# Early ternary of the gate weights inside the first attention, and the tail's weight transposes moved ahead

## The reference, cut to what matters

```
x = x + attention(layernorm(x), ctx, ctx)          # 16 heads, 1024 keys, causal
x = x + mixture_of_experts(layernorm(x))           # 8 experts, top 2, hidden 1024
x = x + quantised_attention(layernorm(x), ctx)     # Wq, Wkv, Wp; all 2048 keys
x = x + ternary_ffn(layernorm(x))                  # w_gate, w_up (2048 x 512), w_down (512 x 2048)

def weight_quant(w):
    s = 1.0 / clip(mean(abs(w)), 1e-5)
    return clip(round(w * s), -1.0, 1.0) / s
```

## Time and profile before

| | us |
|---|---|
| median of 3 runs | 1581.54 |
| lowest, highest | 1578.25, 1591.35 |
| the profiled execution's own time | 1582.63 |
| its span, first to last instruction | 1580.7 |
| busy: PE, DVE, ACT, POOL | 1310.6, 1212.1, 997.3, 335.0 |
| mean granted clock of PE | 0.903 of full speed |

### The profile page before, as it was taken

One profiled execution on the slowest core, in us unless ns is written; L12 is line 12 of the kernel. 1 busy time (PEld: TensorE's weight loads), 2 busy tenths in 40 slices (PEclk: granted clock), 3 DMA queues, 4 the chain that ended last, 5 costly groups with the idle time before them and its releaser, 6 DMA issues.

```text
span 1580.7 us, 24025 instructions
## 1 busy us (share of the span) xinstructions
PE 1310.6 (83%) x8549; PEld 768.5 (49%) x8596; DVE 1212.1 (77%) x1799; ACT 997.3 (63%) x1291; POOL 335.0 (21%) x317
## 2 busy tenths in 40 slices
PE   8992888888865799999999997655777777779886
PEld 3441455555534566666666664313343444444333
DVE  6998899999976655555666664876999999984963
ACT  5775788888853455544455551335889888882574
POOL 1113200000004444445552004001112111110440
PEclk9996999999987899999999999766888778779998
DMA  8996455445344899999999975399887789783001
GB/s 293 288 288 164 94 114 133 121 117 122 79 167 190 327 416 417 414 417 418 415 415 403 354 273 173 65 204 212 174 170 171 162 164 177 164 145 96 1 1 53
DMA packets 453868, 338.65 MB, mean 214 GB/s; under 512 B 367464, under 2 KB 369512, under 8 KB 453136
## 3 DMA queue, kind: packets, MB, share of 16 engines
q1 hardware_dynamic: 439488, 291.31, 63.6%
q0 software_dynamic: 9920, 37.75, 6.3%
q10 hardware_dynamic: 4368, 8.39, 1.4%
HBM read 205.86 MB, written 38.01 MB: 154 GB/s over the span
## 4 chain that ended last, share of the span: by engine, by line
PE 37%; DVE 29%; issue 16%; DMA 7%; ACT 5%; POOL 3%; SPq 2%; POOLq 0%; DVEq 0%; ACTq 0%
DVE arena L2066 12%; PE scores L1137 8%; DMA arena<-in_L_ffn_w 5%; PE bank L1169 4%; PE scores L1236 4%; PE bank L1019 4%; PE scores L1003 2%; DVE arena L1836 2%; PE bank L1283 2%; DVE arena L1822 2%; PE scores L1002 2%; ACT arena L1480 2%; PE scores L1265 1%; PE bank L1381 1%; POOL xs_d L861 1%
## 5 line engine op out<-in xcount | busy, mean ns | idle before, releaser
L2066 DVE TENSOR_SCALAR_CACHE_REDUCE arena<-scores,arena 128x1024 f32<-128x1024 f32 x256 | 314.4, 1279 | 45.2 <-PE scores L1236 44.3
L1920 DVE TENSOR_TENSOR wlo<-raw,whi 128x2048 fp32r<-128x2048 f32 x92 | 219.8, 2409 | 157.8 <-ACT whi L1531 157.8
L1610 ACT ACTIVATE arena<-arena 128x2048 int16<-128x2048 f32 x128 | 273.5, 2149 | 74.9 <-POOL arena L902 39.3
L1236 PE MATMUL scores<-arena 96*128 96x512 bf16 x512 | 193.3, 485 | 85.3 <-DVE arena L2066 77.9
L1531 ACT ACTIVATE whi<-raw 128x2048 fp32r<-128x2048 f32 x92 | 173.2, 1908 | 51.1 <-PE scores L1137 51.1
L1169 PE MATMUL bank<-arena 128*128 128x512 f32 x368 | 163.8, 594 | 4.0 <-DMA arena<-in_L_ffn_w 3.9
L1137 PE MATMUL scores<-whi,xhi 128*128 128x512 f32 x368 | 159.3, 433 | 3.8 <-DVE xlo L1924 2.1
L1137 PE MATMUL scores<-whi,xlo 128*128 128x512 f32 x368 | 146.3, 398 | 0.0
L1137 PE MATMUL scores<-wlo,xhi 128*128 128x512 f32 x368 | 146.2, 397 | 0.0
L1480 ACT ACTIVATE arena<-scores 128x512 f32<-128x512 f32 (+3 forms) x256 | 116.6, 506 | 26.2 <-PE scores L1003 26.2
L1822 DVE TENSOR_REDUCE arena<-scores 128x1 f32<-128x640 f32 (+3 forms) x128 | 127.6, 1018 | 4.8 <-PE scores L980 4.4
(11 more groups left out here) (292 smaller groups left out, 2336.3 us busy)
## 6 DMA issues: line engine op xcount, KB each, us to landing
raw<-in_L_ffn_w SPq DMA_DIRECT2D x92, 1024.0 KB, 13.2
arena<-in_L_ffn_w SPq DMA_DIRECT2D x46, 1024.0 KB, 18.4
arena<-arena SPq DMA_DIRECT2D x32, 256.0 KB, 2.9
kst_d<-arena POOLq DMA_DIRECT2D x16, 384.0 KB, 5.6
tern_d<-arena POOLq DMA_DIRECT2D x12, 512.0 KB, 6.8
arena<-kst_d SPq DMA_DIRECT2D x16, 384.0 KB, 4.0
xs_d<-arena SPq DMA_DIRECT2D x23, 256.0 KB, 2.9
arena<-xs_d SPq DMA_DIRECT2D x22, 256.0 KB, 16.4
```

Source lines behind the costliest of these rows:

```text
L1236: ins = pe.matmul(scores[:, s:s + 512], qhead[h % 2][0:K3, t * P:(t + 1) * P], khead[h % 2][0:K3, s:s + 512], start=True, stop=True)
L1610: act.activation(dst, src, ACT.Exp, bias=ebias[n % SBUFS], scale=-1.0, accum_out=rsum[h % 2][:, t:t + 1]).then_inc(p_ready, 1)
L1920: dve.tensor_tensor(wlo[:, n % SPLITS], raw[:, n % RAWS], whi[:, n % SPLITS].bitcast(F32), ALU.subtract).then_inc(lo_done, 1)
L2066: dve.tensor_scalar(ssb[i][:, s:s + 1024], scores[:, s:s + 1024], nsq[:, h, t:t + 1], None, ALU.mult, ALU.min, accum_out=nmx[i][:, half:ha ...
```

## The change

The first four chunks of the ternary (all of the gate weight) are made in the first attention. Each gets six units: its load is cut into four quarters of 256 KB, two after the last `p2` group of one unit and two after the same group of the next; a unit is left out; then one step of three in each of the next three units. The first load waits for the fourth unit's last group, the last step for the 27th unit's. The other eight chunks stay where they were, behind the scatter.

The transpose of the gate weight is issued once the last expert slot's hidden rows are turned (`h_turned`), the transpose of the up weight behind the key loads that follow `moe_added`; both are gone from the place behind L693.

```diff
-TERN_EARLY = 0
+TERN_EARLY = 4
...
             sp.dma_start(bq_row, bq.partition_broadcast(P)).then_inc(wq_loaded, 16)
 
+            def turn_weights(w):
+                sp.dma_start_transpose(wT[w].rearrange("p o c n -> p (o c) n"), tern_d[w]).then_inc(wT_in, 16)
+
+            sp.wait_ge(h_turned, 2 * SLOTS)
+            turn_weights(0)
...
             sp.wait_ge(moe_added, 3 * NT)
             load_keys(0)
             load_keys(1)
+            turn_weights(1)
...
             load_queries(1)
-            for w in range(2):
-                sp.dma_start_transpose(wT[w].rearrange("p o c n -> p (o c) n"), tern_d[w]).then_inc(wT_in, 16)
             sp.dma_start(wp_sb, Wp.rearrange("(k p) n -> p k n", p=P)).then_inc(wp_loaded, 16)
...
+            def at_unit(u):
+                pool.wait_ge(p2_done, 4 * (TERN_UNIT + u))
+
             def load_chunk(g, chunk):
                 w, c = g // 4, g % 4
-                if w < 2:
+                if g < TERN_EARLY:
+                    for o in range(4):
+                        at_unit(6 * g + o // 2)
+                        pool.dma_start(chunk[:, o * D:(o + 1) * D], w_rows[w][(4 * c + o) * P:(4 * c + o + 1) * P, :]).then_inc(w_in, 16)
+                elif w < 2:
...
             def in_window(g, i):
 
                 if g < TERN_EARLY:
-                    pool.wait_ge(p2_done, 4 * (TERN_UNIT + 3 * g + i))
+                    at_unit(6 * g + 3 + i)
...
-                pool.wait_ge(w_in, 16 * (g + 1))
+                pool.wait_ge(w_in, 16 * (g + 1 + 3 * min(g + 1, TERN_EARLY)))
```

## The result

The changed kernel takes 1573.02 us (median of 7 runs, 1569.15 to 1576.32), the kernel before in the same series 1581.49 (7 runs). The ratio is 0.9939, with a 95% interval of 0.9924 to 0.9954: 9.6 us, or 0.6%, faster. (The two medians are 8.5 us apart; gains are given by the ratios here, and the interval makes this one 7.3 to 12.0 us.) The forecast was 1563.2, and 18.3 us. So about half of the expected gain came, and the time lies at the upper end of the range of 1557 to 1573, 0.02 us past it. The profiled execution has 1573.34 us, a span of 1571.5 and a clock of 0.908.

A forecast was written before the change was run, and what follows sets the result against it. DVE bounds both attentions, PE with the DMA engines the middle of the experts, plus a hole at 1057 to 1078 us. 17.0 + 3.1 - 1.0 - 0.3 - 0.5 = 18.3 us gain off 1581.5: 1563.2 us, range 1557 to 1573.

The forecast's parts named there:

- The hole: Second attention, 1057 to 1078 us: PE and DVE wait behind SP's two weight transposes; moving them gains 17.0 us.
- Less load beside the experts: Expert stage: four fewer ternary chunks return four slots from 20.10 to 19.32 us, gaining 3.1 us.
- Ternary steps in the first attention: POOL's 12 steps of 1.90 us fit a 2.3 us window in DVE's order; cost 0.5 us for all.
- The up transpose behind the keys: Before the queries: SP is free just in time for the first query transpose; cost 0.3 us, bounds 0 and 8.4.
- The gate transpose at the end of the experts: Beside the 16 gathers: the transpose delays the last gather little; cost 1 us, upper bound 8.2.
- B: Only the hole goes: POOL's lighter stream frees nothing and gathers cost 3; gain 13.2 us, 1568.3; chance 0.15.
- A: Query stage: the up transpose delays the queries, price 6.3 us; gain 12, time 1569.5; chance 0.12.
- C: First attention: POOL's 12 steps each hold DVE 1.90 us, 22.8 in all; 4.0 us slower, 1585.5; chance 0.04.

The follow-up runs named there:

- the experiment with the other window: Changed kernel with the gate transpose behind the gathers and each early ternary step released two `p2` groups earlier: 1572.19 us, one run.
- the experiment with two transposes: Changed kernel with both weight transposes issued behind the key loads, before the first query transpose: 1570.11 us, ratio 0.9907.

## Why the prediction was right and wrong

- **The hole: right.** Forecast 17.0 us, measured 16.9 up to the issue of the first probability transpose and 17.2 up to PE's products. That transpose landed in 7.23 us instead of 7.52, and PE's idle time went from 21.19 to 3.63; I had given 4 to 5 for it.
- **Less load beside the experts: right.** 3.1 us forecast, 3.4 by the marks, 3.0 for the whole ternary part alone. The slots that came back are the four between 781 and 862 us. The value chunks' slots moved up by four and keep their excess, as forecast: 701.02 to 780.94 is 79.9 us for four. Eight early chunks returned no more than four, since one collision of a value chunk with DVE cost PE 3.33 us there.
- **Ternary steps in the first attention: right.** 0.5 forecast, 0 to 0.1 measured. The way it was found, a window of 2.3 us in DVE's order against a step of 1.90, holds, and the experiment with the other window gives its worth: 12 to 13 us. By the Trainium skill, "SBUF — State Buffer", Who interferes with whom, DVE's reductions from PSUM don't ask for the shared ports and its subtractions of two SBUF inputs do; the two placings agree (1.90 us a step against 2.58 to 3.04).
- **The up transpose behind the keys: right.** 0.3 forecast, none measured. It took 9.65 us instead of 8.2, so the first query transpose came 2.0 us after DVE's tile was ready (1021.8), but the third was on time again at 1030.93. The slack that the forecast read from the earlier trace rows was enough for 2 us, and the experiment with two transposes shows that 18.5 us of issue are not absorbed.
- **The gate transpose at the end of the experts: wrong, and by nearly the whole miss.** "I take 1" turned out as 12.3 us, and so the upper bound, "all its 8.2 us go in front of the last gather", was too low as well. The step that failed is this: I took 8.2 us, an issue time measured away from the gathers, for what the transpose costs beside them, added it to 15 us of gather work, and found that 23 fit into 24. Already alone the transpose takes 10.0 us to land, and beside the gathers its packets' time does not stay what it was: 9.5 became 20.3, and the gathers' 14.8 became 16.6. That is 36.9 us of packet time where the forecast had counted 23, and the last gather landed after 17.0 us instead of 3.5. The hint was in the earlier trace rows: in the window of the hole the engines, with the two transposes, stand at a share of 1.14 for 271 GB/s, where the experts' loads get 415 out of 1.03. A transfer that fills the engines at so low a rate is not one that fits between others. I read this row for the hole and not as the transpose's price.
- The Trainium skill's rule, that all issuing engines share the same 16 DMA engines and interleave ("DMA: Bandwidth & Descriptors", Issuing engines are not separate DMA queues), is borne out, from POOL's queue and from ACT's: beside loads from either the transpose issues in 16.3 and 16.8 us instead of 8.0. The 1 to 2 us that I worked out by it came from adding times, which is my step and not the rule's.

With 12.3 in place of 1.0, and the other terms as forecast, the sum would be 17.0 + 3.1 - 12.3 - 0.3 - 0.5 = 7.0 us, 1574.5; measured are 9.6 and 1573.0. Of the rivals, B had "the gathers cost 3", on the right place with a quarter of the size. A and C are real mechanisms that this change keeps clear of.

That the time came out at the edge of the range, and not far outside it, is luck. The range reached to 1573 for rivals A and B, which did not act as described, and the forecast's own 1560 to 1567, which was to cover the gathers, was missed by 6 us.

## What to carry to other kernels

Price a DMA transpose beside other traffic by a run of the two together, not by its time alone: look for a high DMA share with low GB/s. Put it where the queues are quiet and nobody waits for a transfer, here under the layer norm behind the last gather, at the cost of one more wait; here that was worth 12.3 us. Work for POOL beside a busy DVE goes behind a semaphore count that opens just before DVE's reductions from PSUM, with its data loaded early enough that this count, and not the load, releases it.

## What the runs showed of the hardware

- A DMA transpose of 2 MB in 8224 packets takes 8.0 us of SP's issue and 10.0 us to land alone, 16.3 and 18.2 beside 2 MB of plain loads, and 26.7 and 34.3 beside 4.2 MB of gathers. The last gather then lands after 17.0 us instead of 3.5; with a plain 2 MB load beside the gathers it is 3.6. In the engines' packet time a transpose and gathers took 12.6 us more together than apart, a transpose and plain loads about 3.5. What in the engines does this (the small packets, or the change between queues) was only argued and is open; a transpose with other packet sizes wasn't tried.
- The issue time of a transpose is not a fixed cost of SP: it went from 8.0 us alone to 16.3 beside loads and 26.7 beside gathers, and SP's next instruction goes out only behind it (9.65 us of issue behind the key loads made the first query transpose 2.0 us late).
- POOL and DVE held each other where a POOL step met a DVE instruction with two SBUF inputs: steps of 2.58 to 3.04 us instead of 1.90 and three subtractions in 4.39 instead of 2.69, or a POOL step of unchanged 1.97 and a subtraction of 2.10 instead of 1.22. Beside reductions from PSUM both kept their times.
- A half of the transpose lands in 12.4 us beside the gathers and costs nothing on the path; the whole lands in 34.3 and costs 12.3 (9.8 in the run without the early ternary). The price is not in proportion to the size, but hangs on what is still in flight at the last gather.
